# A graph attention layer that gathers each edge tile once and rereads it from DRAM, with its maxima in unrolled steps of four tiles

## The reference, cut to what matters

```python
alpha = leaky_relu(alpha_src[row] + alpha_dst[col], 0.2)   # one number per edge and head
amax = segment_max(alpha, col)
ex = exp(alpha - amax[col])
out = segment_sum(xt[row] * ex, col) / segment_sum(ex, col)
```

## Time and profile before

| | us |
|---|---|
| time, median of 3 (lowest to highest) | 21918.94 (21906.18 to 21924.56) |
| time of the profiled execution | 21875.38 |
| its span, first to last instruction | 21873.6 |
| POOL busy | 14143.2 (65%) |
| PE busy | 10234.6 (47%) |
| DVE busy | 6368.7 (29%) |
| ACT busy | 2697.4 (12%) |

### The profile page before, as it was taken

One profiled execution on the slowest core, in us unless ns is written; L12 is line 12 of the kernel. 1 busy time (PEld: TensorE's weight loads), 2 busy tenths in 40 slices (PEclk: granted clock), 3 DMA queues, 4 the chain that ended last, 5 costly groups with the idle time before them and its releaser, 6 DMA issues.

```text
span 21873.6 us, 147184 instructions
## 1 busy us (share of the span) xinstructions
PE 10234.6 (47%) x41175; PEld 7163.9 (33%) x41176; DVE 6368.7 (29%) x12754; ACT 2697.4 (12%) x4406; POOL 14143.2 (65%) x14027
## 2 busy tenths in 40 slices
PE   5214444444477634434444444444444344448744
PEld 2113333333222323323333333333333333334333
DVE  8401111111477632222222222222222222226422
ACT  0001101010155421101000011001011001100010
POOL 5876676766755676676666666666666666660365
PEclk8655555555688755555555556555555565658855
DMA  1111211211100011121212112121211212125412
GB/s 31 9 23 46 46 42 46 42 46 47 13 1 1 2 14 46 46 48 46 45 47 43 51 46 46 46 48 46 46 47 46 48 46 46 46 46 211 188 46 45
DMA packets 555319, 1025.63 MB, mean 47 GB/s; under 512 B 276823, under 2 KB 344031, under 8 KB 529110
## 3 DMA queue, kind: packets, MB, share of 16 engines
q0 software_dynamic: 448640, 761.10, 16.4%
q1 hardware_dynamic: 102595, 256.61, 3.1%
q10 hardware_dynamic: 3600, 1.51, 0.0%
HBM read 767.92 MB, written 248.53 MB: 46 GB/s over the span
## 4 chain that ended last, share of the span: by engine, by line
POOL 35%; another core or an unknown queue 20%; issue 20%; PE 12%; DVE 7%; DMA 3%; ACT 2%; DVEq 1%; ACTq 0%; POOLq 0%; SPq 0%
POOL rows L405 28%; POOL list_f L389 5%; PE ps L1011 4%; PE ps L1101 3%; POOL list_r L389 3%; ACT work L462 2%; PE ps L1055 2%; DMA rows<-table,rows_F 1%; DVE onehot L701 1%; DVE rows L715 1%; DVE peak_tile L816 1%; DMA rows<-table,rows_R 1%; PE ps L1052 1%; PE ps L1017 0%
## 5 line engine op out<-in xcount | busy, mean ns | idle before, releaser
L1011 PE MATMUL ps<-rows,onehot 128*128 128x128 f32 (+1 forms) x22880 | 5352.9, 406 | 8395.6 <-DVE rows L715 4747.5
L405 POOL DMA_INDIRECT rows<-table,rows_F x7040 | 6864.8, 975 | 3332.5 <-issue 2028.8
L1011 PEld LDWEIGHTS ps<-rows,onehot 128*128 128x128 f32 x22880 | 4677.5, 299 | 9555.0 <-issue 7950.5
L405 POOL DMA_INDIRECT rows<-table,rows_R x3520 | 3419.8, 972 | 1630.1 <-issue 995.5
L462 ACT COPY work<-ps 128x1188 f32 x1430 | 1641.9, 1148 | 16874.2 <-remote 9132.3
L701 DVE TENSOR_TENSOR onehot<-iota,list_F 128x512 f32<-128x512 f32 x1980 | 1284.5, 690 | 5973.0 <-ACT work L462 3385.1
L1000 PE MATMUL ps<-naught 128*128 128x396 bf16 x4290 | 1592.9, 505 | 1492.3 <-issue 1491.9
L405 POOL DMA_INDIRECT rows<-rel_table,rows_F x880 | 851.6, 968 | 1261.1 <-DMA rel_table<-list_R 856.3
L389 POOL DMA_INDIRECT list_f<-list_F,work x850 | 1064.6, 1252 | 401.6 <-issue 258.7
L413 POOL DMA_INDIRECT rows<-peak_table,rows_F x880 | 831.3, 945 | 761.7 <-PE ps L1055 534.4
L389 POOL DMA_INDIRECT list_r<-list_R,rows_R x850 | 1110.6, 1307 | 259.0 <-issue 259.0
(11 more groups left out here) (198 smaller groups left out, 6211.3 us busy)
## 6 DMA issues: line engine op xcount, KB each, us to landing
rel_table<-list_R SPq DMA_DIRECT2D x196, 1024.0 KB, 3.9
rows<-table,rows_F POOLq DMA_INDIRECT x7040
rows<-table,rows_R POOLq DMA_INDIRECT x3520
table<-H SPq DMA_DIRECT2D x5, 3136.0 KB
rows<-peak_table,rows_F POOLq DMA_INDIRECT x880
rows<-rel_table,rows_F POOLq DMA_INDIRECT x880
list_f<-list_F,work POOLq DMA_INDIRECT x850
list_r<-list_R,rows_R POOLq DMA_INDIRECT x850
```

The source lines that it names most:

```text
L405: pool.indirect_dma_start(out=rows[:, t % UNROLL, 0:FEAT], out_offset=None, in_=from_table, in_offset=bass.IndirectOffsetOnAxis(ap=rows_of ...
L1011: ins = mm(into, onehot[:, s, :], rows[:, s, 0:width], start=False, stop=True, skip_group_check=True)
```

## The change

Four things change. First, the two tables become one, `gat_table`, whose rows hold 128 features and the 4 words behind them. Second, the peak pass gathers these whole rows (528 bytes). As each quad lands, SP stores it to `gat_rows` in DRAM, 2112 bytes for each partition, and after the pass SP loads quad after quad back into the ring for the sums, so that `block_sums("gat F")` has no gathers on POOL. Third, the peak pass is unrolled: DVE, ACT and PE take four tiles a step, with one operation over 512 columns where there were four over 128, and one maximum over 2048 columns. Fourth, the 470 scatters that stood behind the peak pass and behind the sums (40 and 7 tens) all stand behind the peak pass.

```diff
-PAUSES = {"sage0 F": 9, "sage1 F": 9, "sage2 F": 20, "peak F": 40, "gat F": 7}
+PAUSES = {"sage0 F": 9, "sage1 F": 9, "sage2 F": 20, "peak F": 47}
...
# SP
+                    for q in range(QUADS):
+                        sp.wait_ge(peak_landed[q % QRING], 16 * QUAD * (q // QRING + 1))
+                        sp.dma_start(gat_rows[q], quad_of_rows(q)).then_inc(spilled[q % QRING], 16)
+                    sp.wait_ge(alphas_moved, QUADS)
+                    for q in range(QUADS):
+                        if q < QRING:
+                            sp.wait_ge(spilled[q], 16 * (QUADS // QRING))
+                        else:
+                            sp.wait_ge(quad_summed, quads_before("gat F") + q - QRING + 1)
+                        sp.dma_start(quad_of_rows(q), gat_rows[q]).then_inc(quad_landed["gat F"][q % QRING], 16)
...
# POOL
             def peak_gathers():
-                for t in range(TILES):
-                    if t >= UNROLL:
-                        pool.wait_ge(summed, t + 1)
+                for q in range(QUADS):
+                    if q >= QRING:
+                        pool.wait_ge(spilled[q % QRING], 16 * (q // QRING))
+                        pool.wait_ge(alphas_moved, q - QRING + 1)
...
-            for name in SUMS[:3] + ["peak F"] + SUMS[3:]:
+            for name in SUMS[:3] + ["peak F"] + SUMS[4:]:
...
# ACT
+                for q in range(QUADS):
+                    act.wait_ge(alphas_moved, q + 1)
+                    if q >= 2:
+                        act.wait_ge(peak_summed, q - 1)
+                    for t in range(q * QUAD, (q + 1) * QUAD):
+                        for h in range(HEADS - 1):
+                            ins = nc.scalar.mul(diag[:, t % (2 * QUAD), h, :], ident[:, :], share[:, t, h:h + 1])
+                        ins.then_inc(diag_ready, 1)
...
# PE
+            for q in range(QUADS):
+                pe.wait_ge(peak_members, 3 * q + 2)
+                if q >= 2:
+                    pe.wait_ge(peak_read, q - 1)
+                for t in range(q * QUAD, (q + 1) * QUAD):
+                    mm(ps[:, t % (2 * QUAD), :].rearrange("p (h e) -> p h e", h=HEADS), absent[:, t % (2 * QUAD), :],
                        never.unsqueeze(1).to_broadcast([P, HEADS, P]), start=True, stop=False)
+                pe.wait_ge(peak_members, 3 * q + 3)
+                for t in range(q * QUAD, (q + 1) * QUAD):
+                    pe.wait_ge(diag_ready, t + 1)
+                    ins = mm(ps[:, t % (2 * QUAD), :], onehot[:, t % (2 * QUAD), :],
+                             diag[:, t % (2 * QUAD), :, :].rearrange("p h e -> p (h e)"), start=False, stop=True)
+                ins.then_inc(peak_summed, 1)
```

More of the change, by code:

```diff
@@ L240, in gnn_kernel @@
         sums_clear = sem("sums_clear")
-        landed = [sem(f"landed{s}") for s in range(UNROLL)]
+        peak_landed = [sem(f"peak_landed{q}") for q in range(QRING)]
+        spilled = [sem(f"spilled{q}") for q in range(QRING)]
         quad_landed = {name: [sem(f"quad_landed_{name.replace(' ', '_')}_{q}") for q in range(QRING)] for name in SUMS}
@@ L283, in windows_before, with quad_of_rows, quad_there, blocks_of_tiles @@
             return WINDOWS * SUMS.index(name)
+        def quad_of_rows(q):
+            return rows[:, q % QRING * QUAD:(q % QRING + 1) * QUAD, :].rearrange("p t f -> p (t f)")
+        def quad_there(name, q):
+            return 16 * (1 if name == "gat F" else QUAD) * (q // QRING + 1)
         def table_at(eng, name):
             eng.wait_ge(table_written, 16 * (TABLES.index(name) + 1 + (TABLES.index(name) >= 3)))
+        def blocks_of_tiles(engine, t):
+            _, values = nc.values_load_multi_w_load_instructions(
+                block_of[0:1, t:t + UNROLL], engines=(engine,), min_val=0, max_val=BLOCKS - 1,
+                skip_runtime_bounds_check_because="each is a count of BLOCKS - 1 comparisons")
+            return values
         def blocks_of_body(engine, i):
@@ new lines, in peaks_of, with between @@
+            def peaks_of(q):
+                dve.wait_ge(peak_summed, q + 1)
+                v.tensor_reduce(peak4[:, q % 2, :], ps[:, q % 2 * QUAD:(q % 2 + 1) * QUAD, :].rearrange("p k (h e) -> p (k h) e", h=HEADS),
+                                AX, ALU.max).then_inc(peak_read, 1)
+            for q in range(QUADS):
+                if q >= 2 and (q - 2) % QRING == 0:
+                    blk = blocks_of_tiles(mybir.EngineType.DVE, (q - 2) * QUAD)
+                def between(j):
+                    if q >= 2:
+                        peak_largest(q - 2, j, blk[(q - 2) % QRING * QUAD + j])
+                peak_operands(q, between)
+                between(3)
+                if q >= 1:
+                    peaks_of(q - 1)
@@ L820, in _ @@
+            for q in (QUADS - 2, QUADS - 1):
+                for j in range(QUAD):
+                    peak_largest(q, j, blk[q % QRING * QUAD + j])
+                if q == QUADS - 2:
+                    peaks_of(QUADS - 1)
+            dve.wait_ge(peak_added, TILES)
             dve.wait_ge(table_written, 16 * 5)
@@ L955, in _ @@
             pe.sem_inc(chunk_summed, CU)
-            pe.sem_inc(summed, UNROLL)
             pe.sem_inc(turned, 2)
```

123 lines of the change are left out of this document (52 added, 71 removed).

## The result

The change makes the kernel faster: 20829.73 us (median of 4 runs, 20798.3 to 20846.01) against 21921.75 us of before (21906.18 to 21931.07). The ratio is 0.9503, 95% interval 0.9492 to 0.9515. The forecast was 20720 us with a range of 20560 to 21380. The profiled execution took 20846.01 us, span 20844.2.

The account below looks back on a forecast made before the run. POOL's gathers were taken as the bound. Savings of 392 (peak pass), 151 (gap), 599 (sums), 53 (end) and 1 (rounding) make 1196 us: 20680 profiled, plus 43.6 for the median, forecast 20720 us, range 20560 to 21380.

Parts of the forecast that it names:

- Start unchanged: Peak pass: it starts as before, the large table being issued at the same point; first gather at 5853.3 us.
- Peak pass 1230, from 5.5 us a quad: Unrolled peak pass: 220 quads at 5.5 us plus 20 for the tail, 1230 us, 392 less than before.
- DVE in POOL's way, 0.5 a quad: Peak pass: about one gather a quad takes 1.43 instead of 0.94 us beside DVE's operations, raising 4.98 to 5.5.
- Stores at nothing: Peak pass: SP's quad stores cost nothing under the ring's slack of over 15 us; without it up to 5.6 a quad.
- Share pass 447: Share pass: nothing changes but names of semaphores, so it stays at 447 us.
- The gap goes, the scatters are covered: Between share pass and sums: 151 us go; 470 scatters, 736 us, hide under share pass and sums, 1117 us.
- Sums 670, from 6.0 a window: Sums of gat F on loads: 6.0 us a window, 660 plus 10 for the ends, 670 us, 599 saved.
- End 58 + 13: Layer's end: norm unchanged at 58 us, then 13 us from the next table to its first gather; 53 saved.
- Holes that stay: Rival, chance 0.22 at least in part: unexplained delays remain, sums 609 us longer, peak pass 48 longer, 21380 us in all.
- Blocked gathers at 6.8 a quad: Rival, chance 0.09: DVE's three operations each stop POOL for their whole length; peak pass 1516 us, 286 more, total 21010.
- Loads that do not overlap: Rival, chance 0.03: each load in the sums waits for the quad just summed, 8.9 us a quad, 22010 us, slower.
- POOL as the bound behind its scatters: Rival, chance 0.01: POOL's scatters end after the sums and set the time; they would need 2.5 us each.

Follow-up runs that it names:

- e1: Changed kernel with the unrolled peak pass kept but the single gather undone (16-byte gathers, gat F gathers again); 19588.29 us, ratio 0.9892 to before beside it.
- e2: Gather-once part alone: before's looped peak pass, with 528-byte gathers, SP's stores and loads for the sums; 19037.51 us, ratio 0.9615 to before beside it.
- e5: The changed kernel itself, timed again on another chip beside before; 18800.6 us against 19824.65, ratio 0.9485.
- e9: The changed kernel itself, timed a third time in another group beside before; 18765.23 us against 19789.66, ratio 0.9482.
- e7: Changed kernel without 216 of its 220 stores, the loads reading the last four quads again and again; 18801.22 us, ratio 0.9484 to before beside it.
- e3: Changed kernel with PE's part of the peak pass as a loop over pairs of quads instead of straight-line code; 18784.18 us, ratio 0.9488 to before beside it.

## Why the prediction was right, step by step

- *Start unchanged.* It came 51 us later, but e1, e2 and e5 start within 7 us of each other, and at the first place the layers ahead were already slower in after than in before, with the same code.
- *Peak pass 1230, from 5.5 us a quad.* Measured 1438 at the first place, 6.5 a quad, and 1152 where no semaphore is late, 5.2 a quad. This is the step that failed. The engines' rates were right or close: POOL 4 x 1.289 = 5.16 (I had 4.98 to 5.5), DVE 4.69 from one maximum to the next when it waits for nothing (4.9), ACT 12 x 0.387 = 4.64 (4.7), PE busy for 987 / 220 = 4.49 in e5 and 4.94 at the first place (4.3, which was low). What failed is that I had excluded late semaphores in this pass and put them at nothing: the text on record says that the old pass shows no holes of that kind. It does show them, shorter ones; the lines below are ACT's and POOL's waits there. The new pass gathers more densely, and DVE alone stands 295 us in them. The 286 us between the two places go with them. That gathers are their condition at the first place, and dense ones the more, is only argued: "remote" waits are absent in its sums on loads and in its share pass, although scatters run beside both, and present in every stage of it that gathers. What they are stays open: nothing but before and the changed kernel ran at the first place.

```profile
ACT work L477 <- remote: 78.1, 32, 7.4
...
POOL rows L413 <- remote: 43.9, 28, 3.0
```

- *DVE in POOL's way, 0.5 a quad.* 0.15 in e9; at the first place, where a gather's mean is 1026 ns, 0.32. It was sized too high.
- *Stores at nothing.* Shown by e7.
- *Share pass 447.* 448.
- *The gap goes, the scatters are covered.* They end 290 us before the last copy; I had about 400 before anyone needs POOL, and it was 363 (8424.98 - 8062.3).
- *Sums 670, from 6.0 a window.* 570 measured, 5.1 a window. The mechanism was right, the holes went with the gathers, and the size was off: the 5.98 us had been read at PE's half clock, and when nothing stood any more PE had the faster one, 0.87 instead of 0.58. My own lower bound, 5.02 a window, was the right row to read.
- *End 58 + 13.* 8411.07 - 8353.1 = 58.0, and 13.9 to the first gather.
- *Sum.* 1196 expected inside the layer, 1094 measured: 208 too little saved in the pass, 100 too much feared in the sums. The end gave 8 more than expected, and the share pass and the rounding make up the rest of these 102. With the 51 and 13 us from outside, the profiled execution took 166 us more than the 20680 forecast for it. Two things about medians took 56 of that back: 40 us had been added for the median, and this profiled execution lies 16 us above its own. So the forecast came out 110 us low. That it lies so near is in part luck: the errors of the pass and of the sums have opposite signs.
- *Rivals.* Holes that stay: true of the peak pass, where I had priced them at 48 us, and false of the sums. Blocked gathers at 6.8 a quad: refuted as a cause by e5, where the same operations run and a quad takes 5.2; at the first place its 6.5 would have looked like it. Loads that do not overlap: no, a quad of the sums takes 2.55 us, half a window of 5.10, against 8.9. POOL as the bound behind its scatters: no, they end 363 us before POOL is needed.

The split, where before takes 19797 us: 208 us from unrolling, 759 from gathering once (gap 151, sums 567, scatters at the end 47, less some 14 in the looped pass; the last 8 are not assigned), and 45 (e3) to 57 (e5, e9) more together than apart. e5 and e9 were timed in other groups, so this last term is known to some 30 us. Most of it is the pass, which takes 1191 us with narrow gathers (mean 1030 ns) and 1152 with wide ones (984). Why a gather of 16 bytes is the slower one beside DVE's quads stays open.

## What to carry to other kernels

When POOL's gathers set the pace, ask whether a stage gathers what another gathers again; stores and loads of whole tiles by SP cost nothing here. A rate read at a low granted clock is not the rate of the same chain once its stalls are gone. Before a mechanism is built on waits for which the trace names no releaser, run the kernel before on another chip: here a tenth of the time went with them, from 21922 to 19797 us, with the program unchanged.

## What the runs showed of the hardware

The same kernel took 21922 us at one place and 19790 to 19825 us on four chips afterwards, and neither is one disturbed run: the runs of each agree within 0.3%. What differs in the traces are waits for PE's semaphores beside POOL's gathers: 55 waits, up to 9.4 us, in one pass of 1438 us. Whether that chip differs, or a state of it, no run here tells. The ratio of the change was all but the same at both, 0.9503 and 0.9485 (0.9469 to 0.9501), since where they occur the pass gains less (184 us against an estimated 247, 1399 less 1152) and the sums more (699 against 567).
